# Sum and score scatters of the edge loop in another order on GpSimd, with the loads and merges behind them

## The reference, cut to what matters

```
h_e = einsum('nf,hfd->hnd', x, W_e); h_r = einsum('nf,hfd->hnd', x, W_r)   # 8 heads, d = 64
diff = h_r[:, dst] - h_r[:, src]
score = s_src + s_dst + einsum(diff, a_dif) + einsum(abs(diff), a_abs) + einsum(hr_src * hr_dst, a_prd)
alpha = leaky_relu(score, 0.2)                  # per head and edge
ex = exp(alpha - segment_max(alpha, src)[src])
att = ex / (segment_sum(ex, src)[src] + 1e-16)
out = segment_sum(att * h_e[dst], src)          # 625 x 512
```

## Time and profile before

| | |
|---|---|
| three runs | 2196.59, 2193.5, 2197.24 us; median 2196.59 |
| profiled execution | 2197.39 us, span of its trace 2195.6 us |
| busy | TensorE 95%, VectorE 47%, ScalarE 33%, GpSimd 25% of the span |
| edge loop | about 99 to 358 us |
| quantisation | about 358 to 396 us |
| heads | about 397 to 536 us |
| TensorE's granted clock | mean 0.98 of full speed |

### The profile page before, as it was taken

One profiled execution on the slowest core, in us unless ns is written; L12 is line 12 of the kernel. 1 busy time (PEld: TensorE's weight loads), 2 busy tenths in 40 slices (PEclk: granted clock), 3 DMA queues, 4 the chain that ended last, 5 costly groups with the idle time before them and its releaser, 6 DMA issues.

```text
span 2195.6 us, 21978 instructions
## 1 busy us (share of the span) xinstructions
PE 2077.8 (95%) x8164; PEld 1261.8 (57%) x8164; DVE 1041.9 (47%) x2151; ACT 724.6 (33%) x1226; POOL 557.2 (25%) x475
## 2 busy tenths in 40 slices
PE   6998898799999999999999999999999999999998
PEld 3575565688666655545665665665565444444443
DVE  8886767787664433474543554454345200000002
ACT  2576655677432200032432432342241111111110
POOL 4577774443320100112022012003002200122202
PEclk9999999799999999999999999999999999999999
DMA  9622211831021111111011011011010877777822
GB/s 343 196 31 30 30 14 36 218 92 61 33 86 59 58 67 42 39 63 68 10 63 68 10 58 69 13 58 63 0 58 28 306 278 301 295 296 302 300 108 76
DMA packets 61524, 237.49 MB, mean 108 GB/s; under 512 B 23351, under 2 KB 28427, under 8 KB 39292
## 3 DMA queue, kind: packets, MB, share of 16 engines
q1 hardware_dynamic: 31914, 168.27, 21.4%
q0 software_dynamic: 26336, 62.19, 9.3%
q10 hardware_dynamic: 3168, 5.63, 0.7%
HBM read 204.07 MB, written 31.96 MB: 108 GB/s over the span
## 4 chain that ended last, share of the span: by engine, by line
PE 74%; DVE 13%; issue 5%; DMA 3%; POOL 2%; ACT 2%; PEldq 0%; PEld 0%; ACTq 0%; DVEq 0%; SPq 0%; POOLq 0%
PE PS L759 10%; PE PS L752 10%; PE PS L1054 10%; PE PS L1485 7%; PE PS L1494 7%; PE PS L1523 7%; PE PS L1097 2%; PE PS L1364 2%; PE PS L1281 2%; DMA pair_scores<-TS,SIDX 2%; PE PS L904 2%; PE PS L1384 2%; PE PS L1385 2%; POOL pair_scores L2105 2%; PE PS L1263 1%
## 5 line engine op out<-in xcount | busy, mean ns | idle before, releaser
L2075 POOL TENSOR_TENSOR RSTD<-VE,HALF 125x1 f32<-125x1 f32 x100 | 81.4, 814 | 943.8 <-DVE VE L2246 943.8
L1054 PE MATMUL PS<-XT,WR 128*128 128x500 f32 (+2 forms) x992 | 232.1, 391 | 8.5 <-ACT XT L1591 3.5
L904 PE MATMUL PS<-HR,HOT 125*125 125x512 f32 x800 | 211.8, 413 | 24.1 <-DVE HOT L2392 24.1
L3132 DVE TENSOR_TENSOR AR<-AR,PS 128x512 f32<-128x512 f32 (+1 forms) x44 | 30.2, 687 | 404.6 <-PE PS L1494 402.3
L759 PE MATMUL PS<-WR,XT 128*125 128x512 f32 x424 | 194.6, 606 | 0.9 <-DVE AR L2909 0.9
L1054 PEld LDWEIGHTS PS<-XT,WR 128*128 128x128 f32 x992 | 143.8, 191 | 86.7 <-issue 70.6
L904 PEld LDWEIGHTS PS<-HR,HOT 125*125 125x125 f32 x800 | 146.8, 191 | 66.8 <-DVE HOT L2392 26.1
L2094 POOL DMA_INDIRECT pair_sums<-CW,SIDX x80 | 136.5, 1706 | 52.6 <-DMA pair_sums<-CW,SIDX 27.0
L759 PEld LDWEIGHTS PS<-WR,XT 128*125 128x125 f32 x424 | 79.0, 192 | 87.0 <-issue 83.4
L2035 ACT ACTIVATE AR<-PS 128x512 f32<-128x512 f32 (+1 forms) x44 | 26.3, 597 | 299.1 <-PE PS L1485 299.1
L752 PE MATMUL PS<-XT,WR 128*128 128x313 f32 (+3 forms) x432 | 122.8, 441 | 1.3 <-DVE CW L2356 0.8
(11 more groups left out here) (457 smaller groups left out, 3918.1 us busy)
## 6 DMA issues: line engine op xcount, KB each, us to landing
WR<-in_qkv SPq DMA_DIRECT2D x12, 1024.0 KB
WR<-in_omm SPq DMA_DIRECT2D x12, 1024.0 KB
pair_scores<-CNT SPq DMA_DIRECT2D x1, 12212.0 KB
AR<-pair_scores SPq DMA_DIRECT2D x5, 2187.5 KB
AR<-in_x_a SPq DMA_DIRECT2D x10, 1024.0 KB, 9.8
AR<-in_x_b SPq DMA_DIRECT2D x10, 1024.0 KB, 5.0
AR<-in_x_c SPq DMA_DIRECT2D x10, 1024.0 KB, 7.2
WR<-in_x_a SPq DMA_DIRECT2D x8, 1024.0 KB, 9.2
```

The source lines that it names most:

```text
L904: last = mm(DIFF[m % 4], HOT[g % 2][0:P, k, tile(j)], HR[0:P, k, :, b, :], start=(k == 0 and b == 0), stop=(k == NT - 1 and b == 1))
L1054: last = mm(by_tile(s)[:, t0:t1, :], w[:, k, 128 * m:128 * (m + 1)], XT[:, k, P * t0:P * t1].rearrange("p (c n) -> p c n", n=P), start=(k ...
L2075: g.tensor_tensor(RSTD[:, t:t + 1], VE[:, t:t + 1], HALF[:, :], ALU.pow)\
```

## The change

- On GpSimd 16 sums instead of 20 go ahead of the first score, 54 are spread over the 80 scores (none or one behind each), and ten stand behind the last.
- SyncE loads the scores of tile 0 first, as soon as the last score scatter has landed, and waits for the sum scatters behind that.
- The merges of counts go behind heads: VectorE merges tile 0 after the first four maxima and tiles 1 to 4 at heads 0, 1, 3 and 6; GpSimd at heads 2, 3, 4, 6 and 8.
- ScalarE waits for the last score instead of the spread factors before the quantisation; VectorE makes the factors after the second group of the quantisation and the joins after the fourth.

```diff
--- before.py
+++ after.py
@@ -39,7 +39,8 @@
 STEPS = 10
 MARKS = ET // STEPS
 BEYOND = float(2 ** 20)
-LEAD = 20
+LEAD = 16
+SUMS_BEHIND = 10
 SCORES_AHEAD = 8
 WIDE_ROWS = (0, 112, P)
 EXPERTS = 8
@@ -582,8 +583,6 @@
                     sp.wait_ge(hot_built, 5 * 2 * (j - 1))
                     edge_ids(j)
 
-            for b in range(2):
-                sp.wait_ge(sums_scattered[b], 16 * ET // 2)
             def sums_of(t):
                 for b in range(2):
                     for lo, hi in zip(WIDE_ROWS, WIDE_ROWS[1:]):
@@ -596,12 +595,14 @@
                     sp.dma_start(TSC[t % 2][lo:hi], pair_scores[N * (P * t + lo):N * (P * t + hi), :].rearrange(
                         "(p q) h -> p (q h)", q=N)).then_inc(pairs_in[t % 2], 16)
 
+            sp.wait_ge(diff_filled, ET)
+            sp.wait_ge(scattered, 16 * ET)
+            scores_of(0)
+            for b in range(2):
+                sp.wait_ge(sums_scattered[b], 16 * ET // 2)
             sp.wait_ge(edge_read, GROUPS)
             sp.wait_ge(graph_filled, 1)
             sums_of(0)
-            sp.wait_ge(diff_filled, ET)
-            sp.wait_ge(scattered, 16 * ET)
-            scores_of(0)
             sp.wait_ge(scaled_ready, 1)
             sums_of(1)
             sums_of(2)
@@ -1733,7 +1734,7 @@
                         done[0] += len(groups)
                     yield
 
-            act.wait_ge(uv_ready, 5)
+            act.wait_ge(score_ready, ET)
             ahead = quantized(0)
             for t in range(NT):
                 for rows in (HRT_LOW, HRT_HIGH):
@@ -2106,11 +2107,15 @@
                     out=pair_scores, out_offset=bass.IndirectOffsetOnAxis(ap=SIDX[:, m:m + 1], axis=0),
                     in_=TS[:, m % SCORES_AHEAD, :], in_offset=None).then_inc(scattered, 16)
 
-            for m in range(ET + LEAD):
-                if m < ET:
-                    add_sums(m)
-                if m >= LEAD:
-                    put_scores(m - LEAD)
+            among = ET - LEAD - SUMS_BEHIND
+            for m in range(LEAD):
+                add_sums(m)
+            for m in range(ET):
+                put_scores(m)
+                for s in range(LEAD + m * among // ET, LEAD + (m + 1) * among // ET):
+                    add_sums(s)
+            for m in range(ET - SUMS_BEHIND, ET):
+                add_sums(m)
 
             def signed(u):
                 for k, (j, c, width) in enumerate(groups_of(u)):
@@ -2135,12 +2140,11 @@
                 one, two = SUMS_IN[t]
                 g.tensor_tensor(G[:, t, :], one[:, :, 1], two[:, :, 1], ALU.add).then_inc(weights_merged, 1)
 
-            merge(0)
             for k in range(NT * HEADS0):
                 t, h = divmod(k, HEADS0)
                 product(k)
-                if k in (0, 1, 4, 7):
-                    merge((0, 1, 4, 7).index(k) + 1)
+                if k in (2, 3, 4, 6, 8):
+                    merge((2, 3, 4, 6, 8).index(k))
                 if h == 6 and t:
                     add_heads(t - 1)
                 if h == 1 and t > 1:
@@ -2478,14 +2482,16 @@
                 onehot(m + 3)
             tile_scores(ET)
             dve.wait_ge(score_ready, ET)
-            step(v.tensor_scalar(UP[:, :, :], U[:, :, :], -0.8, None, ALU.mult))
-            for lo in (0, DH0):
-                rows = slice(lo, lo + DH0)
-                v.tensor_tensor(
-                    SPREAD[rows, :, :].rearrange("p h (b d) -> p h b d", b=2),
-                    ID[rows, rows].unsqueeze(1).unsqueeze(1).broadcast_to([DH0, HEADS0, 2, DH0]),
-                    PRODUCT[rows, :].unsqueeze(2).unsqueeze(3).broadcast_to([DH0, HEADS0, 2, DH0]),
-                    ALU.mult).then_inc(uv_ready, 1)
+            def spread_factors():
+                step(v.tensor_scalar(UP[:, :, :], U[:, :, :], -0.8, None, ALU.mult))
+                for lo in (0, DH0):
+                    rows = slice(lo, lo + DH0)
+                    v.tensor_tensor(
+                        SPREAD[rows, :, :].rearrange("p h (b d) -> p h b d", b=2),
+                        ID[rows, rows].unsqueeze(1).unsqueeze(1).broadcast_to([DH0, HEADS0, 2, DH0]),
+                        PRODUCT[rows, :].unsqueeze(2).unsqueeze(3).broadcast_to([DH0, HEADS0, 2, DH0]),
+                        ALU.mult).then_inc(uv_ready, 1)
+
             def quantized(u):
 
                 groups = groups_of(u)
@@ -2518,13 +2524,16 @@
                     yield
 
             ahead = quantized(0)
-            dve.wait_ge(graph_taken, 1)
-            for k, part_ in enumerate((EA1[0:DH0, :], PS[0:DH0, 2 * BANK:2 * BANK + N])):
-                v.tensor_tensor(EA2[0:DH0, :], EA2[0:DH0, :], part_, ALU.add).then_inc(graph_joined, 1)
-                dve.wait_ge(graph_joined, k + 1)
             for t in range(NT):
                 psum.skip(T=2)
                 next(ahead)
+                if t == 1:
+                    spread_factors()
+                if t == 3:
+                    dve.wait_ge(graph_taken, 1)
+                    for k, part_ in enumerate((EA1[0:DH0, :], PS[0:DH0, 2 * BANK:2 * BANK + N])):
+                        v.tensor_tensor(EA2[0:DH0, :], EA2[0:DH0, :], part_, ALU.add).then_inc(graph_joined, 1)
+                        dve.wait_ge(graph_joined, k + 1)
 
             def left(u):
 
@@ -2590,12 +2599,10 @@
             left(1)
             for _ in ahead:
                 pass
-            merge(0)
             for k in range(4):
                 raw_scores(k)
                 shift(k)
-                if k % 2:
-                    merge(1 + k // 2)
+            merge(0)
             turned_counts(0)
             counted(0)
             for k in range(NT * HEADS0):
@@ -2608,8 +2615,8 @@
                     counted(k + 1)
                 if k + 4 < NT * HEADS0:
                     shift(k + 4)
-                if k in (1, 6):
-                    merge(3 + k // 6)
+                if k in (0, 1, 3, 6):
+                    merge((0, 1, 3, 6).index(k) + 1)
                 if h == 4:
                     turned_counts(t + 1)
                 if h == 6:
```

## The result

The changed kernel took **2208.97 us** (median of 19 runs, 2198.85 to 2214.20), the kernel before 2199.15 us beside it (19 runs, 2192.53 to 2211.56). The ratio is 1.0031 with a 95% interval of 1.0017 to 1.0045: slower by 0.3%, where 3.2 us less had been forecast. The profiled execution of the changed kernel took 2201.8 us, its span is 2200.0 us against 2195.6, and TensorE's mean granted clock in it is 0.974 against 0.980.

A forecast was written before the change was run, and what follows sets the result against it. GpSimd's scatter queue was taken to set the edge loop's pace; last score scatter 362.9, plus 29.5 for sums and 31.6 for loads, put the ninth maximum at 424.3 against 427.54, so 2196.59 - 3.2 = 2193.4 us, range 2182 to 2203.

The forecast's parts named there:

- Part 1, the loop: Edge loop, GpSimd's scatters: 53 intervals at 3.58 and 26 at 2.80 put the last score scatter at 362.9 us, 16 sooner.
- the 13 tail intervals at 2.53: Scores scattered alone at the old loop's end, up to 357.14 us; their average supported 2.80 for intervals without a sum.
- Part 2, the sums behind: Eleven sums after the last score scatter: landed 29.5 us later, at 392.4 us; bounds 24 and 42.
- My estimate of over 9 us: Sums beside the score load: by the skill's packet rule one takes over 9 us, making the sums behind 31, not 29.5.
- Part 3, the loads: SyncE's loads after the sums: 31.6 us without a gap, so the ninth maximum starts at 424.3 us, 3.2 sooner.
- the six microseconds of slack: Kernel before: second score load read as ending at 421.4 us, VectorE's ninth maximum starting at 427.54.
- Part 4, at no cost: Quantisation: starts 1.5 us sooner, 4.5 us of VectorE work moves between groups with about 4 covered; comes out at zero.
- the yardstick: VectorE's ninth maximum, 427.54 us in the kernel before; behind it both kernels were said to do the same work.
- the sums behind would be held up: Rival behind the last score: the score load slows five more sums to 4.7 us, 9.5 slower, 2206.1 us; chance 0.14.
- Freely running scatters: Rival in the loop: 26 intervals at 2.53 and eleven sums at the lead's pace, 13 us sooner, 2183.4; chance 0.32.
- scores that free nothing: Rival in the loop: landing waits keep the 26 intervals at 3.14, 5.6 us slower than before, 2202.2; chance 0.12.
- The rival given 0.06: No effect: VectorE and ScalarE cannot use the freed scatters, or a later wait eats all; 2196.6 us, chance 0.06.

The follow-up runs named there:

- the quantisation alone: The kernel before with only the sooner start of ScalarE's quantisation, factors and joins moved between its groups; 2205.21 us, ratio 1.0023.
- After delayed: The changed kernel with three extra small VectorE operations at the end of the heads' loop; 2197.33 us, ratio 1.0000.
- before delayed: The kernel before with five extra small VectorE operations at the end of the heads' loop; 2199.07 us, ratio 0.9993.
- all spread: The changed kernel with each sum of the loop ahead of its score, none behind the last, and merges sooner; 2189.34 us, ratio 0.9961.
- spread alone: The kernel before with LEAD 16 and each later sum ahead of its score; loads, merges and quantisation as before; 2187.55 us, ratio 0.9954.
- sums loaded first: The changed kernel with SyncE's order as before: sums of tile 0 loaded ahead of its scores; 2223.98 us, ratio 1.0090.

## Why the prediction was wrong

- **Part 1, the loop: near, with a miscount in it.** The first score scatter came at 98.03, with the offset of 1.7 at 99.8, where 100.4 was forecast. The 53 intervals with a sum took 3.49 us on average (3.58 said), the 26 without 2.90 (2.80 said, bounds 2.35 and 3.14). 98.03 + 185.0 + 75.4 = 358.4; forecast 362.9. The last reduction at 334.98 was forecast at 338. But from 109.43 to 324.24 us lie 59 intervals and not 60, so a pair took 3.64 us before and not 3.58. With 3.64 the 53 intervals cost 3.2 us more, the last score scatter comes at 366.1 and the ninth maximum at 427.5, where it was. The whole saving of 3.2 us came from this slip; by its own terms the sum says no change. Also, the 13 tail intervals at 2.53 were the quick ones (all twenty average 2.73), and the scatter at 326.80 stood behind a score and not straight behind a sum.
- **Part 2, the sums behind: right place, size too small.** 34.4 us instead of 29.5. I had two sums delayed to 9 and 13 us by the load; the trace has one that waits 11.14 us, to 16.2. My bounds were of a pace per sum, and no sum that waits out the whole load was among the cases. The Trainium skill, "DMA: Bandwidth & Descriptors", section on queues, rings and completion order, says that an engine goes round its queues packet by packet, and puts some 9 to 17 descriptors in a packet. My estimate of over 9 us for a sum under the load took every row as a packet, which the page does not say. It is nearer the trace than my own two delayed sums, but that is luck: the first sum, issued until 361.23, had landed by 374.5, some 13 us later, because it landed with the end of the load and the load took 11.8 us and not 9. How the engines shared their turns, no run here shows.
- **Part 3, the loads: nearly right.** From the sum loads' issue to the ninth maximum 33.2 us instead of 31.9. The term that was mis-sized is the score load, 9.2 us. In the DMA records of after the second one's 125 packets run from 413.54 to 425.21, 11.7 us; the four sum loads take 20.5 (21.2 said). In before they run from 412.15 to 424.62. I had read the end at 421.4 in the earlier trace rows, where only a new load begins to share the engines (sums of tile 4, issued at 421.13), so the six microseconds of slack ahead of the ninth maximum were three. The second score load of after went out at 412.62, as the third merge of VectorE ended (410.49 + 2.11, I had such merges at 0.80); the last packets of tile 3's sums end at 414.26, so that cost little. Together 358.4 + 34.4 + 33.2 = 426.0, where 424.3 had been said: 1.7 us off, and with the offset 3.5. The saving of 3.2 us up to there wasn't found: 0.3 us more from the first sum scatter, 1.8 less from the first matmul to the 2400th. Of the signs listed, the last sum landed later (34.4 us, 27 to 33 said), the first merge waited longer (13.06 us, 3 to 9 said), and the sums behind went out 3.0 us apart on average, at the limit named as wrong; the ninth maximum at 426.06 is inside 420 to 428.
- **Part 4, at no cost:** right as far as the traces tell: 0.8 us by the run with the quantisation alone, no more than traces differ there, and under the loads' waits in the change itself.
- **The step that failed** is the yardstick, the sentence that behind the ninth maximum both kernels do the same work, with nothing put down for it. They do, and it isn't the same time: 1672.0 us against 1664.4. I read TensorE's clock in the windows of the loop and not behind it, where the page of before has stretches of lower clock in its profile too (30.1 us). With the mean clock beside the times, the sum should have had a term for it: 6 us for the stretch of 20.5 (20.0 against 14.1 us for the same matmuls), 7.6 with the two shorter ones, in either direction. That is more than the 3.2 us forecast, and the range up to 2203 left it out. It bears on the timed medians too: 9.8 us between them is about 11 by the clock and 2 the other way.
- **The rivals.** That the sums behind would be held up was right in place, and never came to its 37 us; its 2206.1 is near the measured time by luck, through another cause. Freely running scatters and scores that free nothing were both off: 2.90 lies between 2.53 and 3.14. The rival given 0.06, in its form that a later wait eats all, is what happened up to the ninth maximum; the time it gave, 2196.6, was not.

**What is shown and what is open.** Shown: in the traces the loss is not in the parts that the change touches; it lies at stretches of lower clock, and the time goes with the clock run by run; one program has both pictures; a kernel with none of the change has the stretch too. Not shown: that a small shift brings or removes a stretch, which is theory C in full. After delayed points that way (3 of 12 runs at low clock against 19 of 31), before delayed doesn't. Not settled: why after is at the low clock in 19 of 31 runs and before in 6 of 111. The two long stretches have fixed places in the code; what decides whether it comes was not tried by itself.

## What to carry to other kernels

Don't leave accumulating scatters behind the point at which a large load starts on the same DMA engines: spread them between the scatters of the loop, so that the one which releases the load is the last of all. Before work is held back to end a loop sooner, count what waits for the held-back part (here all merges and every load but the first). For changes under half a per cent, compare the time at the lower clock and matmuls of the same number first; two profiles of one and the same program differed by 6.4 us (after) and by 8.2 us (all spread) behind the 2400th matmul, and a ratio of that size says little of the change itself. And count intervals, not events: one pair too many made up the whole forecast gain here.

## What the runs showed of the hardware

- An accumulating scatter of sums held the second one behind it for 11.14 and 11.69 us (after and its repeat) when a score load ran beside it. The load's packets took 11.8 and 12.0 us from first to last there, and 11.3 to 12.5 us for the first two score loads of before, all spread and spread alone, with no scatter beside them, so the scatter waited for the load and did not visibly slow it. Without the load the gap was 0.30 (sums loaded first).
- VectorE's addition of two 125x625 tiles took 0.80 us alone and 2.11 and 2.35 beside GpSimd's. The GpSimd row below runs until 419.70, VectorE's (started 418.02) ends 0.67 us after it, and the merge at 410.49 also ends 0.67 us after GpSimd's, so VectorE stood still until GpSimd was through. The other way round, GpSimd's first took 2.40 instead of 1.81 with VectorE's started at 400.26. The Trainium skill, "SBUF — State Buffer", section on its terms, has this as a port pair that one of the two holds for an instruction while the other is blocked; the trace agrees.

```profile
400.31 2.40 POOL L2141 TENSOR_TENSOR G<-Y 125x625 f32<-125x625 f32 x1 [5.05 <-DMA Y<-pair_sums]
...
417.89 1.81 POOL L2141 TENSOR_TENSOR G<-Y 125x625 f32<-125x625 f32 x1
```

- One program had 33.0 us at the lower clock in one profile and 57.0 in another (all spread). The stretch of over 10 us that begins between 722 and 748 us began at the 3212th to 3214th matmul in all seven profiles that have one. TensorE was busy 9.82 of the 10 us before it in after, so a lack of work right ahead of it isn't what announces it.
